# A fused attention and expert kernel: the experts' stores moved from the setup into the loop, and the rest of the setup rearranged

## The reference, cut to what matters

```python
def _L0_xattn_ref(query, key, value, Wq, bq, Wk, bk, Wv, bv):
    q, k, v = query @ Wq.T + bq, key @ Wk.T + bk, value @ Wv.T + bv
    return softmax(q @ k.T / 16) @ v

def _L0_ffn_ref(x, ...):
    xln = _ln(x, ln1_w, ln1_b)
    state = xln @ Ws
    x = x + sigmoid(xln @ Wr) * (xln @ Wv) @ Wo
    h = _ln(x, ln2_w, ln2_b)
    conf = sigmoid(h @ [conf_rwkv, conf_trans])
    bids = conf * capital_shares * sigmoid(h @ w_diff) + h @ W_aff
    winner = argmax(bids)                     # expert 0, expert 1 or the gated one
    rwkv[e] = square(relu(h @ K[e])) @ V[e]   # two experts, 256 -> 1024 -> 256
    trans = h @ W1 * sigmoid(state @ W2) @ W3
    return x + select(winner, rwkv, trans) * scale

x = x + _L0_xattn_ref(_layernorm(x), ctx_768, ctx_768, ...)
x = x + _L0_ffn_ref(_layernorm(x), ...)
x = x + _L1_xattn_ref(_layernorm(x), ctx_768, ...)   # ternary weights, int8 activations
x = x + _L1_ffn_ref(x, ...)                          # token shift, sigmoid(r) * (relu(k)**2 @ W_v)
```

## Time and profile before

| what | value |
|---|---|
| median of three runs | 1672.72 us (1668.34 to 1673.26) |
| the profiled execution's own time | 1659.42 us |
| its span | 1657.7 us |
| PE busy | 1386.5 us (84%) |
| DVE busy | 1169.8 us (71%) |
| ACT busy | 946.9 us (57%) |
| POOL busy | 338.2 us (20%) |
| DVE's first instruction of the loop | 88.82 us |

### The profile page before, as it was taken

How to read it: one execution, slowest core, us unless ns; L and a number is a source line. 1 busy time by engine, 2 the same in 40 slices (tenths; PEclk the granted TensorE clock), 3 DMA queues, 4 the chain that set the end, 5 groups by cost and what they waited for, 6 DMA issues and landing times. The chain is left out here.

```text
span 1657.7 us, 26244 instructions
## 1 busy us (share of the span) xinstructions
PE 1386.5 (84%) x8305; PEld 1099.2 (66%) x8347; DVE 1169.8 (71%) x3025; ACT 946.9 (57%) x1433; POOL 338.2 (20%) x309
## 2 busy tenths in 40 slices
PE   7526688899999999999999978828877969999996
PEld 2214576778888888888888867716652237777775
DVE  5523547677777777877778675417988968898885
ACT  3212345555666566665657535438957147887873
POOL 1100111121102212021120110047500033344330
PEclk9857877999999999999999999968988979999998
DMA  6920012355445544545445566533300011111111
GB/s 174 335 61 18 32 63 82 120 171 168 131 133 177 178 131 156 171 147 172 158 151 194 179 225 201 193 111 104 86 13 0 0 39 39 65 57 57 61 53 39
DMA packets 115447, 192.50 MB, mean 116 GB/s; under 512 B 18256, under 2 KB 84384, under 8 KB 115296
## 3 DMA queue, kind: packets, MB, share of 16 engines
q1 hardware_dynamic: 97408, 146.70, 28.0%
q0 software_dynamic: 13664, 43.28, 7.5%
q10 hardware_dynamic: 4256, 1.07, 0.3%
HBM read 134.10 MB, written 57.98 MB: 116 GB/s over the span
## 5 line engine op out<-in xcount | busy, mean ns | idle before, releaser
L1238 ACT ACTIVATE hr_r<-pair 128x512 f32<-128x512 f32 x136 | 80.6, 594 | 174.5 <-PE pair L159 173.9
L157 PE MATMUL pair<-kv_ring,hr_lo 128*128 128x256 f32 x544 | 159.0, 292 | 9.8 <-DVE hr_lo L3180 7.9
L158 PE MATMUL pair<-kv_ring,hr_hi 128*128 128x256 f32 x544 | 155.3, 285 | 0.0
L159 PE MATMUL pair<-kv_ring,hr_hi 128*128 128x256 f32 x544 | 155.0, 285 | 0.0
L157 PE MATMUL pair<-th_hi,kv_ring 128*128 128x512 f32 x272 | 117.3, 431 | 34.5 <-issue 30.9
L4380 POOL DMA_INDIRECT ff<-x_scratch,slots x64 | 90.6, 1415 | 241.8 <-POOLq L3859 141.1
L1044 POOL DMA_INDIRECT rows_scratch<-row,slot x64 | 64.3, 1004 | 324.3 <-DVE slot L3119 263.4
L4400 ACT ACTIVATE ff<-pair,hbs,s1h 128x512 f32<-128x512 f32 x128 | 95.6, 774 | 53.6 <-PE pair L4470 49.0
L157 PEld LDWEIGHTS pair<-kv_ring,hr_lo 128*128 128x128 f32 x544 | 105.6, 194 | 17.3 <-DVE hr_lo L3180 11.2
L159 PE MATMUL pair<-th_hi,kv_ring 128*128 128x512 f32 x272 | 110.7, 407 | 0.0
L158 PE MATMUL pair<-th_lo,kv_ring 128*128 128x512 f32 x272 | 110.1, 405 | 0.0
(11 more groups left out here) (409 smaller groups left out, 4217.5 us busy)
## 6 DMA issues: line engine op xcount, KB each, us to landing
kv_ring<-expert_scratch SPq DMA_DIRECT2D x136, 512.0 KB, 3.7
acc_s<-rows_scratch SPq DMA_DIRECT2D x17, 528.0 KB, 5.0
xn_s<-rows_scratch SPq DMA_DIRECT2D x17, 512.0 KB, 4.4
x_scratch<-acc_s SPq DMA_DIRECT2D x17, 512.0 KB, 5.1
text_scratch<-text SPq DMA_DIRECT2D x17, 512.0 KB, 4.0
expert_scratch<-expert_space POOLq DMA_DIRECT2D x2, 4096.0 KB, 17.8
x_in<-in_x SPq DMA_DIRECT2D x16, 512.0 KB, 4.9
out<-ff SPq DMA_DIRECT2D x16, 512.0 KB, 2.9
```

The costliest lines, as they stand in the source:

```text
L157: pe.matmul(dst, st[1], mv[0], start=start, stop=False, skip_group_check=True)
L158: pe.matmul(dst, st[0], mv[1], start=False, stop=False, skip_group_check=True)
L159: return pe.matmul(dst, st[0], mv[0], start=False, stop=stop, skip_group_check=True)
L1238: s.activation(hr_r[:, c % 2, :], up_ps[:, (c % 2) * T:(c % 2 + 1) * T], ACT.Relu).then_inc(relu_done, 1)
```

## The change

- **Experts' stores.** POOL no longer stores the experts in the setup. The two stores of 4 MB are issued in the loop, right after `pow0(0)`.
- **Zeros.** The four stores of zeros go ahead of POOL's sixth reduction, and SP waits for them at the end of the setup.
- **Values.** `values(q)` uses a stationary of 128 rows, which is two batches at once. There are two groups instead of four, `values_out` adds the bias over 128 partitions, and each group is stored by two DMAs.
- **x.** The tile `x_in` is allocated outside the setup, and batch 0 is loaded by SP behind the second `load_expert`.
- **First uses.** POOL runs one power on a dummy tile at the end of its setup. ACT runs one activation on a dummy operand ahead of its first wait.
- **First wait.** `cols` (the biases) no longer counts into `ctx_loaded`, which starts PE and DVE, but into `image_loaded`.
- **Product W2s.** The product of `ws` and `w2` comes ahead of the turns of `kf` on PE.
- **Orders.** Some neighbours in the loop's lists are exchanged on every engine, most of them around batch 8 with tile 5 and batch 13 with tile 10.

```diff
+        x_in, x_loaded = sb("x_in", [P, NT, C]), loop_sem("fr_x_loaded")
...
-            CTX_LOADED, IMAGE_LOADED, KEYW_LOADED = 16 * 5, 16 * 4, 16 * 5
+            CTX_LOADED, IMAGE_LOADED, KEYW_LOADED = 16 * 4, 16 * 5, 16 * 5
...
-                            sp.dma_start(cols[:, :], a["cols"]).then_inc(ctx_loaded, 16)
+                            sp.dma_start(cols[:, :], a["cols"]).then_inc(image_loaded, 16)
...
                     sp.wait_ge(big_used, 1)
                     load_expert(1)
+                    sp.dma_start(x_in[:, :, :], x_v[0]).then_inc(x_loaded, 16)
                     def store_values(q):
                         sp.wait_ge(val_out, q + 1)
-                        sp.dma_start(vs_dram[4 * q:4 * q + 4].rearrange("b s c -> s b c"), v_two[:, q % 2, :, :]).then_inc(vs_stored[q % 2], 16)
+                        own = slice(4 * q, 4 * q + 4)
+                        for h in range(2):
+                            sp.dma_start(vs_dram.rearrange("(j h) s c -> h s j c", h=2)[h][:, own, :],
+                                         v_all[h * S:(h + 1) * S, own, :]).then_inc(vs_stored, 16)
...
-                    store_values(2)
                     sp.wait_ge(key_t_ready, 2)
...
-                    store_values(3)
-                    for h in range(2):
-                        sp.wait_ge(vs_stored[h], 32)
+                    sp.wait_ge(vs_stored, 64)
+                    sp.wait_ge(zero_stored, 16 * NT)
                     sp.wait_ge(key_stored, 96)
...
+                        if (kind, k) == ("max", A_VIS):
+                            for q in range(NT):
+                                g.dma_start(zero_dram[q * P:(q + 1) * P, :], zrow[:, :]).then_inc(zero_stored, 16)
...
-                    for e in range(2):
-                        g.wait_ge(big_used, e + 1)
-                        g.dma_start(exp_dram[...], space[...]).then_inc(exp_stored, 16)
...
+                    g.memset(warm[:, :], 1.0).then_inc(p_set, 1)
+                    g.wait_ge(p_set, 15)
+                    g.tensor_tensor(warm[:, :], warm[:, :], neg_half, ALU.pow)
...
-                    values_out(2)
                     split_low(1)
-                    values_out(3)
...
-                    s.wait_ge(ctx_loaded, CTX_LOADED)
+                    s.wait_ge(p_set, 7)
+                    s.activation(tcur[0:1, 0:1], ones[:, 0:1], ACT.Identity, bias=0.0)
+                    s.wait_ge(image_loaded, IMAGE_LOADED)
...
-                        for b in range(4):
-                            n = 4 * q + b
-                            pe.matmul(dst, ctx[:, 0, n * S:(n + 1) * S], wv[:, 0, :], start=True, stop=False)
+                        for j in range(4):
+                            own = slice((4 * q + j) * P, (4 * q + j + 1) * P)
+                            pe.matmul(dst, ctx[:, 0, own], wv[:, 0, :], start=True, stop=False)
...
                     def load_x(b):
-                        after(sp, x1_done, b)
+                        if b == 0:
+                            return
+                        sp.wait_ge(x1_done, b)
...
+                    load_expert(4)(5)
+                    load_rows(6)
                     store_text(4)
                     load_sums(5)
-                    load_rows(6)
                     load_small(10)
-                    load_expert(4)(5)
...
                         g.tensor_tensor(rs0[:, :], var0[:, :], neg_half[:, :], ALU.pow).then_inc(rs0_done, 1)
+                        if b == 0:
+                            for e in range(2):
+                                g.dma_start(exp_dram[...], space[...]).then_inc(exp_stored, 16)
...
-                    down(7)(4)
+                    up(0)(5)
                     pe.wait_ge(fm1_done, 18)
                     trans_down(7)
-                    up(0)(5)
...
```

More of the change, by code:

```diff
@@ L402, in values_out @@
                         v.wait_ge(key_done, K_VALUES + q)
[L403 to L406, removed]
-                        for b in range(4):
-                            last = v.tensor_tensor(v_two[:, q % 2, b, :], (out_ps, up_ps)[q % 2][0:S, b * C:(b + 1) * C],
-                                                   bv_row[0:S, :], ALU.add)
+                        v.wait_ge(ms_stored, 32)
+                        for j in range(4):
+                            last = v.tensor_tensor(v_all[:, 4 * q + j, :], (out_ps, up_ps)[q][:, j * C:(j + 1) * C], bv_row, ALU.add)
                         last.then_inc(val_out, 1)
@@ L541, in values @@
                             pe.wait_ge(key_out, 3)
-                        if q >= 2:
-                            pe.wait_ge(val_out, q - 1)
-                        for b in range(4):
-                            n = 4 * q + b
-                            dst = (out_ps, up_ps)[q % 2][0:S, b * C:(b + 1) * C]
-                            pe.matmul(dst, ctx[:, 0, n * S:(n + 1) * S], wv[:, 0, :], start=True, stop=False)
-                            m = pe.matmul(dst, ctx[0:D - P, 1, n * S:(n + 1) * S], wv[0:D - P, 1, :], start=False, stop=True)
+                        for j in range(4):
+                            own = slice((4 * q + j) * P, (4 * q + j + 1) * P)
+                            dst = (out_ps, up_ps)[q][:, j * C:(j + 1) * C]
+                            pe.matmul(dst, ctx[:, 0, own], wv[:, 0, :], start=True, stop=False)
+                            m = pe.matmul(dst, ctx[0:D - P, 1, own], wv[0:D - P, 1, :], start=False, stop=True)
                         m.then_inc(key_done, 1)
@@ L560, in _ @@
                         m.then_inc(key_lin, 1)
-                    values(2)
+                    pe.wait_ge(val_out, 1)
+                    for c in range(2):
+                        for j in range(2):
+                            m = pe.matmul(out_ps[:, c * C:(c + 1) * C], ws[:, j, c * P:(c + 1) * P], w2[:, j, :],
+                                          start=(j == 0), stop=(j == 1))
+                    m.then_inc(key_done, 1)
                     pe.wait_ge(p_set, 12)
@@ L567, in _ @@
                         m.then_inc(key_turned, 1)
[L568 to L574, removed]
             stack.pop()
@@ L625, in build @@
             ones_f, w_part = sb("ones_f", [P, P]), sb("w_part", [P, 8])
-            x_loaded, small_loaded, scattered, gap_zeroed = (loop_sem("fr_" + n) for n in (
-                "x_loaded", "small_loaded", "scattered", "gap_zeroed"))
+            small_loaded, scattered, gap_zeroed = (loop_sem("fr_" + n) for n in ("small_loaded", "scattered", "gap_zeroed"))
             (ve0_ready, rs0_done, nm0_done, xn0_done, turn0_done, fm0_done, scores_done, shift_done, exp_done, tprob_done,
@@ L923, in _ @@
                     load_expert(5)(10)
+                    load_x(15)
                     load_expert(6)(10)
-                    load_x(15)
                     load_expert(7)(10)
@@ L1084, in _ @@
                     pow0(9)
+                    scatter(7)
                     pow3(4)
-                    scatter(7)
                     pow2(8)
@@ L2475, in _ @@
                     state(8)
-                    up(2)(5)
+                    down(0)(5)
                     pe.wait_ge(gate_done, 9)
                     turn_probs(9)
-                    up(3)(5)
+                    up(1)(5)
+                    up(2)(5)
                     pe.wait_ge(t2_done, 9)
@@ L2500, in _ @@
                     pe.wait_ge(fm2_done, 18)
+                    bids_first(8)
+                    up(7)(5)
+                    bids_last(8)
+                    pe.wait_ge(fm2_done, 18)
                     trans_up(0)(8)
-                    up(7)(5)
+                    down(5)(5)
+                    down(6)(5)
                     pe.wait_ge(tfm_done, 14)
```

205 lines of the change are left out of this document (98 added, 107 removed).

## The result

The changed kernel takes 1645.7 us in the median (1642.7 to 1646.6), against 1670.9 us for the kernel before in the same runs. The ratio is 0.9854, with a 95% interval of 0.983 to 0.9877. That is 25.2 us less; the forecast was 1647.4 us and 25.3 us less. Two further sets of runs of the same kernel gave the ratios 0.984 (0.9796 to 0.9884) and 0.9842 (0.9804 to 0.9881).

A forecast was written before the change was run, and what follows sets the result against it. PE bounds the expert stage; SP's queue, slowed by q0's stores, holds the setup open. 22.8 + 3.8 + 1.7 - 3 = 25.3 us off 1672.7 gives 1647.4 us; range 1637 to 1662 with run spread.

The forecast's parts named there:

- The head of the setup: Setup's start: PE's first matmul about 0.6 us sooner without waiting for `cols`, `kf`'s activation 0.9 us sooner, at 50.9.
- The end of the setup: Border between setup and loop: with q0 silent it comes at 66.0 instead of 88.8 us, 22.8 us gained (17.7 to 23.8).
- The first rival: Setup's stores: small runs, not q0, made SP late; gain only 15.1 us, 1657.6 us; chance 0.09.
- x early and the power early: Batch 0 behind the border: loading x early saves 3.8 us, taking POOL's first-use cost early saves 1.7 us.
- The collision: Loop's start: the experts' stores delay batch 1's x load, 3 us lost (0 to 5).
- `load_small(1)` goes out at S + 19 and has over 15 us: Batch 1's small loads, issued 19 us behind the border S, were given over 15 us.
- The estimate of 5 us: Batch 1's x load waits for whole descriptor groups of the experts' stores: 5 us lost in place of 3.
- The clock: PE's granted clock after the setup's pause: 0.50 again up to the same point of the batches, so 0 us.
- the second rival: First batches: the clock comes back later, another 19.39 us of PE work at 0.50; 9.7 us go, 1657.1 us; chance 0.07.
- 0.50 well into the second batch: A granted clock of 0.50 well into the second batch was listed as a sign that the forecast is wrong.
- The third rival: Loop: it waits for something that doesn't move with its start, so within 5 us of 1672.7; chance 0.06.
- The one of SP's order: Tile 5: `load_rows(6)` waits for batch 7's scatter ahead of expert pieces, PE runs dry; 1652.7 to 1683 us; chance 0.04.

The follow-up runs named there:

- the two experiments on the stores: Changed kernel with the experts' stores back in the setup: 1659.3 us; kernel before with only the experts' and zeros' stores moved: 1657.1 us.
- only the orders: The kernel before with the new orders of the loop and nothing else: 1667.4 us, ratio 0.9993.

## Why the prediction was right, step by step

**The head of the setup.** PE's first matmul starts at 7.16 us instead of 7.76, as forecast. `kf`'s activation starts at 50.98; the forecast was 50.9. The last that it waits for is now DVE's `oscale` and no longer PE's product; both chains moved by about that much. ACT's table load stands at 0.81 us, out of the way.

**The end of the setup.** `kt` ends at 58.61 (forecast 58.7), DVE at 61.84 (61.9), and the border is at 66.69 (66.0), a gain of 22.1 us for 22.8. What failed in the details is the issue of `kv_scratch`: 4.29 us, where 1.9 were taken from `ms_scratch` and below 3 stood as the sign. All four stores of `vs_scratch` are issued straight ahead of it here; with two of them there, in the kernel with only the stores moved, it was 2.46. It doesn't matter, since `kvt_scratch` can only be issued once `kt` is ready at 58.61. The first rival, small stores slow by themselves, is refuted: these 256 B runs land in 6.3 us with q0 silent, against 20.3 in the earlier trace rows, and the two experiments on the stores turn the effect on and off. By the rule of the Trainium skill behind that rival (DMA: Bandwidth & Descriptors, Specifications) less than 512 B doesn't reach the line rate. The traces agree in part: in the kernel before 256 B runs move at 211 to 219 GB/s while `ms_scratch` alone is moving (38.0 to 39.2 us), and in the changed one the experts' stores, with packets of 4 KB, at about 400 GB/s (72 to 84 us). But the 512 B runs of `kvt_scratch` move at 227 GB/s (62.0 to 65.5 us of the changed kernel), so no step is seen at 512 B. Short runs are slow here; it was only not what held SP.

DMA view of the changed kernel, 44 to 67 us:

```profile
q1 hardware_dynamic: 10152, 5.35, 93.8%
...
kv_scratch<-act SPq DMA_DIRECT2D x2, 512.0 KB, 6.3
kvt_scratch<-w_raw SPq DMA_DIRECT2D x4, 256.0 KB, 4.2
```

**x early and the power early.** The forecast was 3.8 + 1.7 = 5.5 us; from the border to PE's first turn it was 11.68 and is 6.04, so 5.6. The sum was right, but not the reading under it. The step that failed is "I read it as a cost of first use: 1.7 us": 1.77 us was only the part of the first power that stuck out behind the wait for x. The whole is 7.1 to 8.2 us there, and the earlier trace rows had it already: 7.93 us of "issue" ahead of that power. So the two terms can't be priced one by one. With the dummy power taken first it brings 1.6 us and the early x then 4.0, close to the forecast; the early x alone brings 0.8 (11.60 and 10.83), and the dummy power then 4.8.

**The collision.** The forecast was 3 us lost, with 0 to 5 as bounds; 4.7 were measured, and the second statistics come 29.5 us behind the border, just above the 25 to 29 named as a sign. The size was off because the price was made of the transfer alone. x is ready to be loaded at 87.26 us (85.60 + 1.66) but issued at 89.96, 2.70 us later, where it was 0.29 us in the kernel before: `load_small(1)` stands ahead of it on SP, and its issues took longer (2.69 and 1.27 us for 1.09 and 0.45), as in the setup while q0 was busy. In the kernel before these two lines were, in SP's timeline:

```profile
113.67 1.09 SPq L701 DMA_DIRECT2D vs<-vs_scratch  x2
114.81 0.45 SPq L702 DMA_DIRECT2D cs<-cs_scratch  x1
```

The step "`load_small(1)` goes out at S + 19 and has over 15 us" looked at when its data are needed and not at what is queued behind it. The transfer then takes 6.27 us for 3.99, 2.3 us more. 2.4 + 2.3 = 4.7. The estimate of 5 us from the Trainium skill's rule on turns between queues (DMA: Bandwidth & Descriptors, Queues, rings and completion order) was for the lateness of the transfer. The transfer was 2.3 us longer, and only together with the issues does it come near 5, so the traces don't bear out that figure; the turns themselves no view shows.

**The clock.** PE's last work of the setup ends at 55.2 us. The granted clock is 1.00 until 58, 0.63 in the two us behind that, then 0.50, and it comes back at 113 us, 12 us behind the second turn, as it did before (136.3, with the turn at 124.10). So 0 was right for this term, and the second rival, that the clock comes back later, is refuted. The sign "0.50 well into the second batch" could not tell the two apart: it is so in both kernels. The third rival, that the lead is absorbed, is refuted by the medians. The one of SP's order is refuted by them too, and by PE, which is idle for 1.9 us in all between the stores of tiles 3 and 5 in the second set (102.16 less 100.24).

**The sum.** 22.1 + 5.6 - 4.7 = 23.1 us at the second turn (124.10 - 101.03). The medians of three sets have 24.1 to 30.4 us. So the forecast of 25.3 was close partly by luck: the terms as measured give 2 us less.

**From the second turn to the end.** Of the 23.1 us, 22.4 are still there when tile 0 is stored (340.26 and 317.82), and 12.9 when tile 16 is (1083.00 and 1070.06). In between, the changed kernel took 752.2 us in this execution and 743.9 in its second set, the kernel before 742.7. The third set took 747.7. The instructions are the same and PE's time for them isn't: 696.3 us for 689.4 in the second set and 689.7 in the kernel before, with a granted clock of 0.97 for 0.98. The second set's rows for this stretch:

```profile
317.34:1061.20 743.86, 689.35 (x4332) 602.66 (x4330) 540.07 (x1616) 438.64 (x741) 115.20 (x100) 0.98 0.53 168
```

So the short lead of the profiled pair is read as the spread of single executions, some 8 us between the sets of the changed kernel. PE's time, with the granted clock, makes 6.9 of the 8.4 us between the first two sets, but not always that much: "only the orders" needs 693.9 us of PE and still takes 743.4. Whether the changed kernel's loop is a few us longer as a rule (743.9 to 752.2 for 742.7 and 743.4) five executions can't tell; the medians, with 24 to 30 us won, speak against a loss of 9. What makes the clock differ between executions stays open.

## What to carry to other kernels

Find the instruction that holds a stage open, and then what fills the resource that it waits for: here stores in short runs waited for room beside 8 MB that the loop first reads at 245 us in the kernel before. When such a transfer is moved, look at which issues are queued ahead of the next critical load, and place it behind that load rather than ahead of it; one power later was worth 4.7 us at the second batch, while a gain in the total is not proven. The time by which a first instruction starts behind its input is only a lower bound of its cost where that cost ran beside the wait for the input; here it was 1.77 us of 7.93, and the gap marked "issue" had the whole. Two edits that each shorten one of two such waits have to be priced together.

## What the runs showed of the hardware

The first power on GpSimd takes 7.1 to 10.9 us from when POOL is free until it starts, with no instruction in the profile for it (7.08 us without the dummy power; 10.90 with the stores in the setup); every later one that had to wait starts within 0.1 us of its input. The Trainium skill (GPSIMD Engine Reference, Instruction dispatch) has approximately 6 us for the first call of a freshly loaded kernel, with no visible instruction. The traces agree with the kind and are 1 to 5 us above the figure. That the power's code is loaded in this time is an inference; no run here shows it.

A DMA issue on SP takes longer while another queue is filling the engines. In the setup four issues of `kvt_scratch` took 23.67 us beside q0's stores and 4.50 without; at batch 1 `vs` took 2.69 us for its two issues in place of 1.09, and `cs` 1.27 in place of 0.45 (the timelines of SP in the two kernels, batch 1).
